# The last layer's dense chain split 8 + 6 + 2 batches, the six inside the last batch's attention slots

## The reference, cut to what matters

```python
xn = ada_ln(x, t_emb, ln1_g, ln1_b, aff1_w, aff1_b)
x = x + mha(xn, xn, xn, sa_qw, ..., sa_ow, sa_ob)      # self attention, 56 keys
x = x + mha(x, u, u, ca_qw, ..., ca_ow, ca_ob)         # cross attention, 1500 context keys, 16 heads of 8
xn = ada_ln(x, t_emb, ln2_g, ln2_b, aff2_w, aff2_b)
h = jax.nn.gelu(xn @ ffn_w1 + ffn_b1, approximate=False)
x = x + (h @ ffn_w2 + ffn_b2)
```

## Time and profile before

| | us |
|---|---|
| median of 3 runs | 1837.49 (1835.42 to 1841.11) |
| the profiled execution, its own time | 1831.49 |
| its span in the profile | 1829.7 |
| PE busy | 1592.6 (87%) |
| DVE busy | 1137.4 (62%) |
| ACT busy | 1029.1 (56%) |
| POOL busy | 659.0 (36%) |
| mean granted TensorE clock | 0.907 of full |

### The profile page before, as it was taken

The page is one execution under the profiler, slowest core; times in us unless marked ns, Lnnn a source line. Parts: engine busy times, 40 slices in busy tenths (PEclk is TensorE's granted clock), DMA queues, the critical chain, the costliest instruction groups (busy, mean ns, idle before and its releaser), DMA issues.

```text
span 1829.7 us, 50325 instructions
## 1 busy us (share of the span) xinstructions
PE 1592.6 (87%) x20495; PEld 996.8 (54%) x20495; DVE 1137.4 (62%) x2324; ACT 1029.1 (56%) x1942; POOL 659.0 (36%) x898
## 2 busy tenths in 40 slices
PE   6888788499999998787999999988877999999985
PEld 4555544156666665443566666555333666666552
DVE  4455443466777777355777777663446777776651
ACT  2344323076777777332667777763532777777662
POOL 4000145145666643444566666411241222222100
PEclk7899999589999999797899999996987999999985
DMA  7222114144666544023445755440024556665320
GB/s 198 55 78 70 34 39 96 39 110 124 160 157 151 132 116 101 1 69 91 117 121 153 165 151 144 116 101 2 1 68 110 133 145 171 151 157 135 78 51 6
DMA packets 192239, 187.43 MB, mean 102 GB/s; under 512 B 60015, under 2 KB 183602, under 8 KB 192018
## 3 DMA queue, kind: packets, MB, share of 16 engines
q1 hardware_dynamic: 190434, 183.23, 39.4%
q10 hardware_dynamic: 1008, 1.05, 0.2%
q0 software_dynamic: 576, 0.02, 0.0%
HBM read 114.46 MB, written 59.88 MB: 95 GB/s over the span
## 4 chain that ended last, share of the span: by engine, by line
PE 68%; ACT 15%; DVE 10%; issue 4%; DMA 2%; POOL 1%; SPq 0%; ACTq 0%; DVEq 0%; POOLq 0%
PE PS L1368 14%; PE PS L1218 8%; PE PS L1394 8%; PE PS L1212 7%; PE PS L1342 5%; ACT q_parts L970 4%; DVE mx L1826 3%; PE PS L1207 3%; PE PS L1049 3%; PE PS L1133 3%; PE PS L1471 2%; ACT v_sb L881 2%; PE PS L1153 2%; ACT cxT L872 2%; PE PS L1124 2%
## 5 line engine op out<-in xcount | busy, mean ns | idle before, releaser
L1826 DVE TENSOR_REDUCE mx<-PS 112x1 f32<-112x500 f32 x1152 | 715.5, 672 | 229.1 <-PE PS L1342 225.6
L970 ACT ACTIVATE q_parts<-PS 125x448 f32<-125x448 f32 x1152 | 563.0, 545 | 141.8 <-PE PS L1394 137.9
L697 POOL CAST k_hi<-k_full 128x500 f16<-128x500 f32 x144 | 89.1, 619 | 648.8 <-issue 589.5
L732 POOL TENSOR_SCALAR cx<-cx,norm_b 125x128 f32<-125x128 f32 x384 | 303.9, 806 | 33.5 <-issue 17.7
L1394 PEld LDWEIGHTS PS<-q_st,k_st 50*125 50x125 f16 x4608 | 185.7, 139 | 222.8 <-ACT q_parts L970 154.2
L1394 PE MATMUL PS<-q_st,k_st 50*125 50x112 f16 x4608 | 261.5, 235 | 38.1 <-ACT q_parts L970 29.1
L1368 PE MATMUL PS<-q_parts,v_sb 125*18 125x112 f32 x9216 | 292.0, 270 | 0.0
L1342 PE MATMUL PS<-k_st,q_mx 50*112 50x500 f16 x1152 | 263.2, 402 | 23.9 <-DMA q_mx<-q_all 18.4
L1368 PEld LDWEIGHTS PS<-q_parts,v_sb 125*18 125x18 f32 x9216 | 218.5, 101 | 55.6 <-issue 43.4
L699 POOL TENSOR_TENSOR k_lo<-k_full,k_hi 128x500 f16<-128x500 f32 x144 | 164.0, 1139 | 21.6 <-POOL k_hi L697 3.0
L881 ACT ACTIVATE v_sb<-PS 125x512 f32<-125x512 f32 x144 | 87.0, 604 | 96.6 <-PE PS L1218 96.5
(11 more groups left out here) (278 smaller groups left out, 2057.8 us busy)
## 6 DMA issues: line engine op xcount, KB each, us to landing
k_st<-k_dram SPq DMA_DIRECT2D x288, 187.5 KB, 3.5
cx<-in_ctx SPq DMA_DIRECT2D x56, 672.0 KB
k_dram<-k_hi SPq DMA_DIRECT2D x288, 125.0 KB, 2.6
k_dram<-k_lo SPq DMA_DIRECT2D x144, 125.0 KB, 2.9
v_sb<-in_ctx SPq DMA_DIRECT2D x8, 672.0 KB
q_mx<-q_all SPq DMA_DIRECT2D x48, 99.8 KB
q_st<-q_all SPq DMA_DIRECT2D x48, 99.8 KB
cx<-in_ctx SPq DMA_DIRECT2D x56, 78.0 KB
```

The lines of the kernel that those rows point to most:

```text
L732: last = pool.tensor_scalar(cx[:, p, c, :], cx[:, p, c, :], norm_b[:, p, 0, c:c + 1], norm_b[:, p, 1, c:c + 1], ALU.subtract, ALU.mult)
L970: act.activation(probs[:, c % RING, u * HR:(u + 1) * HR], PS[0:KC, (2 * c + u) % SC_RING, 0:HR], ACT.Exp).then_inc(sem("exp_done"), 1)
L1826: dve.tensor_reduce(mx[:, r, t:t + 1], PS[0:PW, MX_BANK + u % MX_RING, 0:TK], AX.X, ALU.max)\
```

## The change

The halves become `SPANS`: two halves as before for all other chains, and for the last layer's second half two spans, u = 2 (batches 8 to 13, 336 columns) and u = 3 (batches 14 and 15, 112 columns). The chain of u = 2 gets a step in each of slots 1, 2, 3, 4, 5, 6, 7, 8, 10 and 11 of batch 15; its feed stands on DVE in slot 0. The chain of u = 3 follows alone behind the attention. For u = 2 and 3 DVE, not ACT, squares the centred rows and reads the four hidden products; ACT keeps the square root and the Gelu. The output leaves in three stores instead of two. Its core:

```diff
+SPANS = ((0, HB), (HB, HB), (HB, HB - 2), (B - 2, 2))
-               ("cross", 2, 0), ("cross", 2, 1), ("self", 3, 0), ("self", 3, 1), ("cross", 3, 0), ("cross", 3, 1)]
+               ("cross", 2, 0), ("cross", 2, 1), ("self", 3, 0), ("self", 3, 1), ("cross", 3, 0), ("cross", 3, 2),
+               ("cross", 3, 3)]
...
+            if kind == "var" and u > 1:
+                fed = counted("step_fed")
+            elif kind in ("var", "ffn"):
...
+            done = counted("step_done_act" if kind == "var" or kind == "hid" and u < 2 else "step_done")
...
+LAST_SLOTS = (1, 2, 3, 4, 5, 6, 7, 8, 10, 11)
...
+    if layer == 3:
+        for n, step in enumerate(STEPS["cross", 3, 2]):
+            plan[B - 1, LAST_SLOTS[n]] = step
...
         def hcols(t, u):
-            return t[:, u * HR:(u + 1) * HR]
+            lo, n = SPANS[u]
+            return t[:, lo * T:(lo + n) * T]
...
-            store_rows(1)
-            sp.wait_ge(sem("stored"), 32)
+            store_rows(2)
+            store_rows(3)
+            sp.wait_ge(sem("stored"), 3 * 16)
...
-                elif step.kind == "hid":
+                elif step.kind == "hid" and step.u < 2:
...
-                if step.kind == "mean":
+                if step.kind == "mean" and step.u < 2:
                     act.wait_ge(sem(step.done[0]), step.done[1])
                     act.activation(sq_h, cen_h, ACT.Square).then_inc(sem("step_fed_act"), 1)
                 elif (step.kind, step.arg) == HIDDEN[-1]:
                     act.wait_ge(sem(step.done[0]), step.done[1])
-                    act.activation(hidden, hidden, FFN[step.layer][4]).then_inc(sem("step_fed_act"), 1)
+                    act.activation(span_hidden(step.u), span_hidden(step.u), FFN[step.layer][4]).then_inc(sem("step_fed_act"), 1)
...
-                whole("cross", 3, 1)
+                whole("cross", 3, 3)
...
-                    for j in range(RT // 2):
+                    for j in range(pairs_of(u)):
                         last = mm(PS[0:PW, bank, j:j + 1], sq_h[:, j * PW:(j + 1) * PW], mean_w[:, 0:1], start=True, stop=True)
...
-                        before = CHAIN_MISC[c]
+                        before = CHAIN_MISC.get(c)
...
-                    dve.wait_ge(sem("attn_out"), PAIRS * (layer - 1) + PAIRS // 2 * (u + 1))
+                    dve.wait_ge(sem("attn_out"), PAIRS * (layer - 1) + sum(SPANS[u]) // 2)
...
                 if kind == "hid":
+                    if u > 1:
+                        dve.wait_ge(sem(step.ready[0]), step.ready[1])
+                        dve.tensor_scalar(span_of(hid_h[step.arg], u), src, col(FFN[layer][1], step.arg), None, ALU.add)\
+                           .then_inc(sem("step_done"), 1)
                     return
...
+                    if u > 1:
+                        dve.wait_ge(sem("step_done"), step.done[1])
+                        dve.tensor_tensor(span_of(sq_h, u), cen, cen, ALU.mult).then_inc(sem("step_fed"), 1)
...
+                        if b == B - 1 and c == LAST_SLOTS[0] - 1 and (b, LAST_SLOTS[0]) in plan:
+                            feed(plan[b, LAST_SLOTS[0]])
```

More of the change, by code:

```diff
@@ L139, in chain_steps @@
             fed = None
-            if kind in ("var", "ffn"):
+            if kind == "var" and u > 1:
+                fed = counted("step_fed")
+            elif kind in ("var", "ffn"):
                 fed = counted("step_fed_act")
@@ L317, in build, with span_hidden, out_rows, pairs_of @@
         hidden = w1[:, :, :, :].rearrange("p e k n -> p (e k n)")[:, 0:4 * HR]
+        def span_hidden(u):
+            return hidden.rearrange("p (k c) -> p k c", k=4)[:, :, 0:SPANS[u][1] * T]
         hid_h = [hidden[:, k * HR:(k + 1) * HR] for k in range(4)]
-        out_rows = [t[0:PW, 0:RT // 2 * D].rearrange("p (k d) -> p k d", d=D) for t in A[7:9]]
+        row_tiles = [t[0:PW, 0:RT // 2 * D].rearrange("p (k d) -> p k d", d=D) for t in A[7:9]]
+        def out_rows(u):
+            lo, n = SPANS[u]
+            return row_tiles[lo // HB][:, lo % HB // 2:(lo % HB + n) // 2, :]
+        def pairs_of(u):
+            return SPANS[u][1] // 2
+        def span_of(t, u):
+            return t[:, 0:SPANS[u][1] * T]
         s_mx = sb("s_mx", [T, NH])
@@ L386, in hcols @@
         def hcols(t, u):
-            return t[:, u * HR:(u + 1) * HR]
+            lo, n = SPANS[u]
+            return t[:, lo * T:(lo + n) * T]
         def hbatch(t):
-            return t.rearrange("p (b t) -> p b t", b=HB)
+            return t.rearrange("p (b t) -> p b t", t=T)
         def hspread(k, u):
-            return mod[:, k, HB * u:HB * u + HB].unsqueeze(2).to_broadcast([128, HB, T])
+            lo, n = SPANS[u]
+            return mod[:, k, lo:lo + n].unsqueeze(2).to_broadcast([128, n, T])
         def by_batch(t):
@@ L470, in store_rows @@
                 ge(sp, *STEPS["cross", 3, u][-1].done)
-                sp.dma_start(out.rearrange("b t d -> (b t) d")[u * HR:(u + 1) * HR].rearrange("(k p) d -> p k d", p=PW),
-                             out_rows[u]).then_inc(sem("stored"), 16)
+                lo, n = SPANS[u]
+                sp.dma_start(out.rearrange("b t d -> (b t) d")[lo * T:(lo + n) * T].rearrange("(k p) d -> p k d", p=PW),
+                             out_rows(u)).then_inc(sem("stored"), 16)
             for layer in range(layers):
@@ L919, in evacuate @@
                     act.wait_ge(sem(step.ready[0]), step.ready[1])
-                    act.activation(std8[:, step.u, :], PS[0:PW, bank, 0:RT // 2], ACT.Sqrt,
+                    act.activation(std8[:, step.u % 2, 0:pairs_of(step.u)], PS[0:PW, bank, 0:pairs_of(step.u)], ACT.Sqrt,
                                    bias=eps[0:PW, LNS[step.arg][1]:LNS[step.arg][1] + 1]).then_inc(sem("step_done_act"), 1)
-                elif step.kind == "hid":
+                elif step.kind == "hid" and step.u < 2:
                     act.wait_ge(sem(step.ready[0]), step.ready[1])
@@ L1290, in multiply @@
                 elif kind == "var":
-                    for j in range(RT // 2):
+                    for j in range(pairs_of(u)):
                         last = mm(PS[0:PW, bank, j:j + 1], sq_h[:, j * PW:(j + 1) * PW], mean_w[:, 0:1], start=True, stop=True)
                 elif kind == "spread":
-                    for j in range(RT // 2):
-                        last = mm(PS[:, bank, j * PW:(j + 1) * PW], rstd8[:, u, j:j + 1].to_broadcast([PW, 128]),
+                    for j in range(pairs_of(u)):
+                        last = mm(PS[:, bank, j * PW:(j + 1) * PW], rstd8[:, u % 2, j:j + 1].to_broadcast([PW, 128]),
                                   ident[0:PW, 0:PW], start=True, stop=True)
@@ L1300, in multiply @@
                     for j in range(4):
-                        last = mm(dst, W[f[2]][:, j, :], hid_h[j], start=(j == 0), stop=(j == 3))
+                        last = mm(dst, W[f[2]][:, j, :], span_of(hid_h[j], u), start=(j == 0), stop=(j == 3))
                 elif kind == "q":
@@ L1308, in multiply @@
                 else:
-                    for j in range(RT // 2):
+                    for j in range(pairs_of(u)):
                         last = pe.transpose(PS[0:PW, bank, j * D:(j + 1) * D],
-                                            X[:, u * HR + j * PW:u * HR + (j + 1) * PW], ident[:, :])
+                                            hcols(X, u)[:, j * PW:(j + 1) * PW], ident[:, :])
                 last.then_inc(sem("step_ready"), 1)
@@ L1768, in evacuate @@
                     dve.wait_ge(sem(step.done[0]), step.done[1])
-                    dve.reciprocal(rstd8[:, u, :], std8[:, u, :]).then_inc(sem("step_fed"), 1)
+                    dve.reciprocal(rstd8[:, u % 2, 0:pairs_of(u)], std8[:, u % 2, 0:pairs_of(u)]).then_inc(sem("step_fed"), 1)
                     return
@@ L1781, in evacuate @@
                     else:
-                        dve.tensor_scalar(xh_h, src, bias, None, ALU.add).then_inc(sem("step_done"), 1)
+                        dve.tensor_scalar(xh, src, bias, None, ALU.add).then_inc(sem("step_done"), 1)
                         dve.wait_ge(sem("step_done"), step.done[1])
-                        then(dve.tensor_tensor(hbatch(xh_h), hbatch(xh_h), hspread(gate, u), ALU.mult))
-                        dve.tensor_tensor(xs, xs, xh_h, ALU.add).then_inc(sem("step_fed"), 1)
+                        then(dve.tensor_tensor(hbatch(xh), hbatch(xh), hspread(gate, u), ALU.mult))
+                        dve.tensor_tensor(xs, xs, xh, ALU.add).then_inc(sem("step_fed"), 1)
                 elif kind == "mean":
-                    dve.tensor_tensor(cen_h, xs, src, ALU.subtract).then_inc(sem("step_done"), 1)
+                    dve.tensor_tensor(cen, xs, src, ALU.subtract).then_inc(sem("step_done"), 1)
+                    if u > 1:
+                        dve.wait_ge(sem("step_done"), step.done[1])
+                        dve.tensor_tensor(span_of(sq_h, u), cen, cen, ALU.mult).then_inc(sem("step_fed"), 1)
                 elif kind == "spread":
```

(4 more changed lines are left out.)

8 lines of the change are left out of this document (4 added, 4 removed).

## The result

The first comparison gave a median of 1813.16 us (4 runs, 1803.39 to 1815.76) against 1836.45 us of before (4 runs): ratio 0.9873, interval 0.9829 to 0.9918. That is 23 us less, where 13 were forecast and the range began at 1818. Medians and ratios from here on are of undisturbed runs: seven slow ones, of 1835.54 to 7411.85 us, are left out, and the profile of split_only is of such a run, so only its end is read. The changed kernel's profiled execution took 1815.76 us, its span is 1814.0.

The account below looks back on a forecast made before the run. It took batch 15's unaccompanied attention and the serial chain behind it, both at a lowered clock, as the bound. 20.7 us less behind, 7.4 more in batch 15: 13.3 off 1837.49 gives 1824 us, range 1818 to 1832.

Parts of the forecast that it names:

- Term 1: Chain alone behind the attention, 112 columns for 448: 16.4 us against 37.15, so 20.7 us less.
- Term 2: Batch 15 with ten steps of 336 columns: 19.2 us PE queue plus 6.1 us waits, 25.3 us at full clock.
- Term 3: Clock in batch 15: one fall to the lower level adds 2.9 us, making the batch 28.2 us.
- It will fall once: In batch 15 the clock falls only at the Gelu wait of 2.6 us; the ffn then takes 4.5, not 2.5.
- the 26 to 30 named as a sign of being right: Batch 15, first scores to last values, would take 26 to 30 us if the prediction was right.
- How the numbers follow: Closing section: 1824 us spans 1820 to 1829, with the clock's two rivals 1818 to 1832; faster 0.88, same 0.09, slower 0.03.
- the gain is lost elsewhere: Rival: longer engine programs and lower-clock spells in other stages eat the gain; 1831 to 1838 us, chance 0.07.
- stays low through batch 15: Rival: clock falls in slots 1 to 3 and stays low through batch 15; 1830 to 1832.5 us, chance 0.12.
- never falls: Rival: clock never falls in batch 15 and the alone chain begins at full speed; 1819 to 1821 us, chance 0.15.
- the slower rival: Steps do not overlap batch 15's attention at all, costing 26 us in PE's queue; 1843 us, chance 0.04.

Follow-up runs that it names:

- split_only: The changed kernel with the six-batch chain taken out of batch 15's slots and run behind the attention, ahead of the two-batch chain; 1840.72 us, ratio 1.0031 to before.
- no_tables: The changed kernel with square root and Gelu of batches 8 to 13 replaced by plain copies, so not computing the reference; 1808.47 us, ratio 0.9843 to before.
- again: The changed kernel, unaltered, measured a second time; median 1817.56 us of 11 runs, ratio 0.9929 to before.
- again2: The changed kernel, unaltered, measured a third time; median 1818.90 us of 11 runs, ratio 0.9924 to before.
- null_before: The kernel before, unchanged, compared against itself; median 1834.94 us of 11 runs, ratio 1.0006.
- four_four: The changed kernel with spans of 8, 4 and 4 batches, so batches 12 to 15 run alone at the end; 1820.49 us, ratio 0.9912 to before.

## Why the prediction was right, and where it was wrong

- **Term 1, the chain alone: right, its sum closer than its parts.** 16.4 forecast, 16.5 to 16.6 in three profiles. Within it the single products were dearer (0.76 for 0.67), so that the four hidden steps took 4.7 for 4.2 and spread 1.8 for 1.6. Out was quicker (0.46, the clock was still full), and so was the store: the copy ends at 1811.93, the span 2.1 later (2.6 taken). That these cancel is luck. The Gelu's load is off the chain, as argued.
- **Term 2, the walk at the full clock: right.** 25.3 forecast; 25.4 where the clock was held. Both halves of it hold: PE's queue was put at 19.2 us, and PE is busy 19.17 us in no_tables, at the full clock; the waits stand where they were put, 1.05 + 0.66 us in slot 4 for the 1.9, and 2.59 at the Gelu for the 2.6.
- **Term 3, the clock: wrong in its mechanism, and too small.** "It will fall once" was wrong. It fell at the Gelu, and also behind the square root's wait in slot 4 (from the value pair behind the scores at 1774.71: 1.63, product 1.43). In the changed kernel's first profile batch 15 took 28.4 us, with two short spells; in again and again2 the first spell lasted into the third hidden step, some 10 us, the mean granted clock of batch 15 was 0.78, and it took 30.9 and 30.8 us, outside the 26 to 30 named as a sign of being right. The term was 2.9; it measured 3.0, 5.5 and 5.4. The 3.0 agrees by luck: the fall at the Gelu cost less than forecast (ffn 3.81 for 4.5, and the value pair behind it 0.91, not 1.63), and the fall that wasn't forecast made up for it.
- So the end gained 61.2 - 48.1 = 13.1 us in the first pair of profiles, 13.3 forecast, and 10.6 to 13.1 over all three against the same profile of before. Against null_before's 62.9 it is 12.3 to 14.8. The 13 and 15 us of the repeated comparisons agree with that.
- **The step that failed is "How the numbers follow", the last one.** The scatter of whole runs was put at nothing in the range: 1837.49, the median of three runs, was taken for the kernel's centre, and the range of 1818 to 1832 was made of the two terms' bounds and the clock in batch 15 alone. The same section grants that a measurement can tell only some 5.5 us and doesn't add it; with it the range would have begun at 1812.5. What the runs show in its place: runs of one program lie 23 us apart (before, 35 runs) and 19 (again, 11 runs), with a standard deviation of 6.0 and 6.4; a median of four is then good to some 3.5 us, and the difference of two such medians to some 5 (estimates from these deviations). Before's larger samples have their medians at 1830.65 to 1835.27, 2 to 7 us below the centre taken. The first comparison's 23 us is 8 to 10 more than the repeated ones, and its interval meets theirs only at its edge (0.9829 to 0.9918 against 0.9898 to 0.9960): an unusual draw, and nothing in any profile from batch 15 on holds the other 10 us. 1813.16 lies 5 below the range, the 1817.56 and 1818.90 of the repetitions at its lower edge. The profiled execution of before, 6 us under the median, had hinted at it: I noted the distance and did not widen for it.
- The rival "the gain is lost elsewhere" had the right mechanism, spells of the lower clock in the stages before, and was priced on one side only. Such spells are as apt to add to a gain as to take from it.
- The clock's other rivals: "stays low through batch 15" did not happen in any of three profiles; "never falls" happened only with idle products and in no_tables. Overlap failed nowhere: the slower rival's price of 26 us was the 26.2 that split_only shows for the chain of six, so its price was right and its condition did not come. Its sum 37.15 - 16.4 - 26 is -5.25, not -6; the 1843 us are worked out from -5.25.

## What to carry to other kernels

A serial chain at the end is worth cutting to the part that truly depends on the last data and putting the rest into the slots ahead; its price is read as queue time plus the waits at other engines' turns, and it came out to a few tenths here where the clock held. Where an engine's clock depends on what it did before, cost each stretch at both levels, and look at every wait of a us or two for a fall; filling such waits with idle products paid 3.0 to 5.5 us in batch 15 and 2.6 behind it, in the profiles. And before giving a range, ask how far runs of the unchanged kernel lie apart: three close runs don't show it, and the distance of the profiled execution from their median is a free fourth.

## What the runs showed of the hardware

- The same instructions up to batch 15 (20,159 to 20,161 matmul records) took from 1756.0 to 1775.2 us in thirteen profiles (1786.1 in that of split_only). The mean granted clock up to there was 0.93 in again (1756.9), 0.92 in the changed kernel's first profile (1765.9) and 0.91 in split_only. The time of a run goes with its mean granted clock, 0.919 at 1819.42 us and 0.899 at 1842.35 us.
- PE's wait of 1.05 us ahead of the spread was followed by a fall in all three profiles of the changed kernel, in again and again2 while the spread's own records ran (1.04 and 1.18 us for 0.89); with one idle product of 448 columns in that wait none followed, in three profiles. A longer wait isn't always followed by one: behind the 2.22 us at four_four's Gelu the clock stayed at the upper level. What decides it, these runs don't settle.
- A change of ACT's table costs 1.28 us and nothing behind it, and it is loaded ahead of the wait of the instruction that needs it: at 1771.24 with the square root at 1772.54, at 1801.11 with the Gelu at 1807.97.
